# One-core graph layer: 8 KB adjacency runs, own rows gathered ahead of spilled ones, the spilled product and the eviction moved to the end of the period

## Reference

```python
h = jnp.maximum(_layernorm(x, axis=-1), 0.0)
mask = adj > 0
head = mask / jnp.maximum(jnp.sqrt(jnp.sum(mask * mask, axis=-1, keepdims=True)), 1e-12)
inc = adj + head
out = x + (inc @ h) / jnp.sum(inc, axis=-1, keepdims=True)
```

## Time and profile before

| | us |
|---|---|
| median of 3 runs (1261.79 to 1265.77) | 1264.53 |
| the profiled execution | 1265.03 |
| its span, first to last instruction | 1263.2 |
| busy: PE / DVE / ACT / POOL | 970.4 / 1162.8 / 977.8 / 764.9 |
| mean granted TensorE clock | 0.908 |

### The profile page before, as it was taken

One profiled execution on the slowest core, in us unless ns is written; L12 is line 12 of the kernel. 1 busy time (PEld: TensorE's weight loads), 2 busy tenths in 40 slices (PEclk: granted clock), 3 DMA queues, 4 the chain that ended last, 5 costly groups with the idle time before them and its releaser, 6 DMA issues.

```text
span 1263.2 us, 14630 instructions
## 1 busy us (share of the span) xinstructions
PE 970.4 (77%) x2678; PEld 482.8 (38%) x2678; DVE 1162.8 (92%) x2794; ACT 977.8 (77%) x1903; POOL 764.9 (61%) x745
## 2 busy tenths in 40 slices
PE   0002889988888888888888888798888878878676
PEld 0001334444444434444433444344444434434343
DVE  6679999999999999999998999989999989998972
ACT  6657888898888887888887787788878778876551
POOL 1003666766666667676666666775666667667453
PEclk9999999888889999889988988988899889998698
DMA  9999999999999999999999999999999999999442
GB/s 360 428 421 406 398 402 392 392 394 399 396 391 402 401 399 398 384 401 394 384 398 368 400 398 391 388 395 373 402 400 400 385 382 387 398 399 355 142 143 79
DMA packets 148127, 471.29 MB, mean 373 GB/s; under 512 B 24386, under 2 KB 24386, under 8 KB 143876
## 3 DMA queue, kind: packets, MB, share of 16 engines
q1 hardware_dynamic: 90368, 331.38, 66.9%
q0 software_dynamic: 57664, 138.93, 29.9%
HBM read 490.21 MB, written 33.82 MB: 415 GB/s over the span
## 4 chain that ended last, share of the span: by engine, by line
DVE 45%; DMA 20%; issue 20%; ACT 5%; SPq 5%; another core or an unknown queue 2%; PE 1%; DVEq 0%; ACTq 0%; POOL 0%; POOLq 0%
DMA adj_tile<-in_adj_dram 17%; DVE folded L774 15%; DVE cand_word L779 12%; DVE cand_index L783 5%; DMA gathered_rows<-in_x_dram 3%; SPq L385 2%; ACT junk L569 2%; DVE cand_word L797 2%; SPq L392 2%; DVE cand_index L802 2%; ACT adj_tile L556 2%; SPq L396 1%; DVE ln_stats L757 1%; DVE weights_and_payload L914 1%
## 5 line engine op out<-in xcount | busy, mean ns | idle before, releaser
L488 POOL DMA_INDIRECT gathered_rows<-h_scratch,slot_column x520 | 536.8, 1032 | 265.9 <-issue 161.2
L569 ACT ACTIVATE junk<-adj_tile,zero_unit 128x2048 bf16<-128x2048 f32 x256 | 510.1, 1994 | 111.2 <-issue 75.5
L1330 PE MATMUL acc<-gathered_rows,diag 128*128 128x512 f32 x1040 | 504.1, 641 | 0.5 <-issue 0.5
L488 POOL DMA_INDIRECT gathered_rows<-h_scratch,spill_column x197 | 220.5, 1119 | 199.0 <-ACT spill_column L615 150.8
L774 DVE SCALAR_TENSOR_TENSOR folded<-adj_tile 128x1024 f32<-128x1024 f32 x248 | 301.4, 1215 | 12.1 <-DMA adj_tile<-in_adj_dram 10.7
L1330 PEld LDWEIGHTS acc<-gathered_rows,diag 128*128 128x128 f32 x1040 | 213.7, 212 | 247.1 <-issue 246.8
L779 DVE MAX8 cand_word<-folded 128x8 f32<-128x1024 f32 x248 | 302.9, 1221 | 2.2
L783 DVE FIND_INDEX8 cand_index<-cand_word,folded 128x8 uint32<-128x1024 f32 x248 | 302.2, 1218 | 0.0
L1341 PE MATMUL acc<-gathered_rows,spill_matrix 128*128 128x512 f32 x394 | 186.3, 607 | 14.6 <-issue 10.7
L632 ACT ACTIVATE diag<-ident,weights_and_payload 128x128 f32<-128x128 f32 x582 | 176.2, 387 | 0.5 <-DVE weights_and_payload L914 0.5
L1278 PE MATMUL poff<-spill_rank,lanes_before 128*128 128x1 f32 x130 | 26.4, 272 | 187.5 <-DVE spill_rank L859 174.4
(11 more groups left out here) (146 smaller groups left out, 829.8 us busy)
## 6 DMA issues: line engine op xcount, KB each, us to landing
adj_tile<-in_adj_dram SPq DMA_DIRECT2D x256, 1024.0 KB
h_scratch<-adj_tile SPq DMA_DIRECT2D x16, 1024.0 KB, 10.5
out_dram<-out_tile SPq DMA_DIRECT2D x64, 256.0 KB
gathered_rows<-in_x_dram SPq DMA_DIRECT2D x12, 1024.0 KB, 12.6
x_residual<-in_x_dram SPq DMA_DIRECT2D x48, 256.0 KB
gathered_rows<-h_scratch,slot_column POOLq DMA_INDIRECT x520
x_held<-in_x_dram SPq DMA_DIRECT2D x4, 1024.0 KB, 7.9
gathered_rows<-h_scratch,spill_column POOLq DMA_INDIRECT x197
```

Of the source, the lines that this page charges most:

```text
L488: nc.gpsimd.indirect_dma_start(out=into, out_offset=None, in_=h[:, :], in_offset=bass.IndirectOffsetOnAxis(ap=column, axis=0), bounds_chec ...
L569: nc.scalar.activation(junk[:, n % 2].rearrange("p (j c) -> p j c", j=2), both[:, :, half], ACT.Relu, bias=zero_unit[:], scale=-UP, accum_ ...
L1330: last = nc.tensor.matmul(acc[t % 3][:], diag[:, t % 2, 1 + s], slot(t % 2, s), start=False, stop=False)
```

## The change

Four edits go together.

1. A chunk is now 2048 neighbouring columns, one run of 8 KB a row; the fold adds columns c and c + 1024 of the chunk. Bases, the diagonal's chunk and the order of the parts of an unfolded tile follow from it.
2. GpSimd gathers the own rows of tile T-1 before the spilled rows of tile T-3.
3. In a period TensorE does the own products right after the residual, then offsets, the payload, and the spilled product of tile f last.
4. ScalarE does `row_again` and `own_matrices` before the first check, `reach_places` right after the third, and evicts tile f at the end of the period. The store of a tile stands one period later in SyncE's queue.

The batch now has four spill groups in place of three, and one small step of the final tests is gone. In the last periods the gather of the batch's x rows stands later in GpSimd's list, and the batch period's eviction and spilled product of tile 60 stand later too.

```diff
-    adj_h = adj.rearrange("(c p j) (h n) -> c j p h n", p=P, j=ROWS, h=2)
+    adj_t = adj.rearrange("(c p j) n -> c j p n", p=P, j=ROWS)
...
         def diag_chunk(t):
-            return t // ROWS * P * ROWS % HALF // CW
+            return t // ROWS * P * ROWS // (2 * CW)
...
         def groups(t):
-            return EXTRA if FOLDED <= t < BATCH else FOLDED_EXTRA
+            return EXTRA if wide(t) else FOLDED_EXTRA
...
-                sp.dma_start(chunk(t % 2, j), adj_h[t // ROWS, t % ROWS, :, :, CW * j:CW * (j + 1)]).then_inc(adj_loaded[t % 2][j], 16)
+                sp.dma_start(A[:, t % 2, 2 * CW * j:2 * CW * (j + 1)],
+                             adj_t[t // ROWS, t % ROWS, :, 2 * CW * j:2 * CW * (j + 1)]).then_inc(adj_loaded[t % 2][j], 16)
...
-                if t >= 4:
-                    store_tile(t - 4)
+                if t >= 5:
+                    store_tile(t - 5)
...
-            gather_own(0)
-            gather_own(1)
-            for t in range(2, BATCH + 1):
+            for t in range(BATCH - 1):
...
-                gather_spill(t - 2)
-                if t < BATCH:
-                    gather_own(t)
+                gather_own(t)
+                if t >= 2:
+                    gather_spill(t - 2)
...
                 if pay:
-                    own_matrices(q)
                     if not wide(q):
                         row_again(q)
+                    own_matrices(q)
                 if t == FOLDED + 1:
                     list_rows()
+                check(t, 0)
...
-                if end:
-                    finish_tile(f)
                 if small:
                     reach_places(p)
                 check(t, 3)
+                if end:
+                    finish_tile(f)
...
-                if end:
-                    product_spill(f)
...
                 if pay:
                     residual(q)
+                    product_own(q, 0)
+                    product_own(q, 1)
                 offsets(p)
                 if pay:
                     bring_spill(q)
-                    product_own(q, 0)
-                if pay:
-                    product_own(q, 1)
+                if end:
+                    product_spill(f)
```

More of the change, by code:

```diff
@@ L206, in diag_chunk @@
         def diag_chunk(t):
-            return t // ROWS * P * ROWS % HALF // CW
+            return t // ROWS * P * ROWS // (2 * CW)
         def diag_column(t):
-            k = t // (TILES // 2) * 8 + t % 8
-            return diag_at[:, k:k + 1]
+            return diag_at[:, t % 16:t % 16 + 1]
         def cands(t):
@@ L242, in searched @@
             return CHUNKS * min(t, FOLDED) + PARTS * max(t - FOLDED, 0)
-        def part(i):
-            return i % 2 * CHUNKS + i // 2
         def paid(t, k):
@@ L422, in _ @@
                     load_chunk(t + 2, 3)
-            for t in range(TILES - 4, TILES):
+            for t in range(TILES - 5, TILES):
                 store_tile(t)
@@ L523, in _ @@
                         bounds_check=N - 1, oob_is_err=False).then_inc(batch_adj, 16)
-                    pool.wait_ge(row_added, FOLDED)
-                    nc.gpsimd.indirect_dma_start(
-                        out=again[:], out_offset=None, in_=x[:, :],
-                        in_offset=bass.IndirectOffsetOnAxis(ap=bad_row[:, 0:1], axis=0),
-                        bounds_check=N - 1, oob_is_err=False).then_inc(batch_x, 16)
-                gather_spill(t - 2)
-                if t < BATCH:
-                    gather_own(t)
+                gather_own(t)
+                if t >= 2:
+                    gather_spill(t - 2)
+            pool.wait_ge(row_added, FOLDED)
+            nc.gpsimd.indirect_dma_start(
+                out=again[:], out_offset=None, in_=x[:, :],
+                in_offset=bass.IndirectOffsetOnAxis(ap=bad_row[:, 0:1], axis=0),
+                bounds_check=N - 1, oob_is_err=False).then_inc(batch_x, 16)
+            gather_spill(BATCH - 3)
+            gather_own(BATCH - 1)
+            gather_spill(BATCH - 2)
             gather_spill(BATCH - 1)
@@ L683, in period @@
                     spill_matrix(r)
-                if small:
-                    roots(p)
                 if pay:
@@ L688, in period @@
                 check(t, 1)
+                if small:
+                    roots(p)
                 check(t, 2)
-                if end:
-                    finish_tile(f)
                 if small:
@@ L708, in batch_period @@
                 reach_places(y)
+                finish_tile(u)
                 check_batch(1)
@@ L786, in part_columns @@
             def part_columns(t, i):
-                if t == BATCH:
-                    return A[:, 0, CW * part(i):CW * (part(i) + 1)]
-                return chunk(t % 2, part(i) % CHUNKS)[:, part(i) // CHUNKS]
+                return A[:, t % 2, CW * i:CW * (i + 1)]
             def part_values(t, i):
@@ L794, in part_values @@
                 else:
-                    dve.wait_ge(adj_loaded[t % 2][part(i) % CHUNKS], 16 * turn(t))
-                e = slice(8 * part(i), 8 * part(i) + 8)
+                    dve.wait_ge(adj_loaded[t % 2][i // 2], 16 * turn(t))
+                e = slice(8 * i, 8 * i + 8)
                 nc.vector.max(out=cv[:, t % 2, e], in_=part_columns(t, i)).then_inc(vals_found, 1)
@@ L1177, in mark_rows @@
                                                     scalar=float(PLACES), in1=w_well[:, 5], op0=ALU.is_le, op1=ALU.add))
-                step(nc.vector.scalar_tensor_tensor(out=w_well[:, 6, TILES - FOLDED:], in0=end_all[:, BATCH:BATCH + 1],
-                                                    scalar=float(FOLDED_EXTRA * P),
-                                                    in1=w_well[:, 5, TILES - FOLDED:], op0=ALU.is_le, op1=ALU.add))
                 step(nc.vector.tensor_scalar(b_mark[:, FOLDED:], w_well[:, 6, 0:TILES - FOLDED], 4.5, None, ALU.is_lt))
@@ L1391, in batch_period @@
                 product_own(w, 1)
+                product_spill(u)
                 find_owner(y)
```

11 lines of the change are left out of this document (4 added, 7 removed).

## The result

The change makes the kernel slower: 1402.96 us in the median of 4 runs (1394.59 to 1408.27) against 1264.97, a ratio of 1.109, 95% interval 1.1032 to 1.1148. I had predicted 1259 us, and the range ended at 1281. The profiled execution of the changed kernel took 1394.59 us, its span is 1392.9.

What follows compares the result with a forecast made beforehand. VectorE bounds tiles 3 to 19, transfers plus payload waits tiles 20 to 60. With the new ring setting the period, +3.0, -9.4, -0.6 and +1.1 us give -5.9 from 1265.0: 1259 us, range 1244 to 1281.

Steps and rivals of the forecast that it cites:

- The ring: Loop from TensorE's spilled product through ScalarE's eviction, row_again and own_matrices to TensorE's next products; floors every period, taken as 17.15 us.
- The two ends are 16.2 and 17.35. I take 17.15: Ring length with TensorE at full rate, with its whole clock loss inside, and the value chosen near the upper end.
- The loss to TensorE's clock: TensorE's time at 1.2 GHz in the ring: about 1.15 us a period, not all of it counted.
- The handover from TensorE to ScalarE: From TensorE's last spilled pass to ScalarE's eviction in the ring; the ring's sum gave it no time.
- The long waits of `find_entry`: VectorE's waits for TensorE's payload, three in tiles 20 to 60, 13 us together; expected to be gone.
- The slack: Limits stand ready before VectorE reads them at pay_places: 5.0 us, spent once, taken off tiles 3 to 19.
- 8 KB runs: Adjacency loads: 0.31 us less per tile, bounds 0 and 0.5; transfers' pace in tiles 20 to 60 from 17.07 to 16.76.
- Rival C: Own-row gathers held back by longer runs: 0.4 us late a period, ring 17.55, about 1283 us; chance 0.08.
- Own rows first on GpSimd: Own gathers start up to 3.9 us earlier, spilled ones some 10 to 12 us later; no cost.
- Rival B: The ring binds with TensorE's whole clock loss: 17.45 us a period, 1276 us, slower; chance 0.20.
- the forecast: Ring near 17.15 us sets the period, time 1248 to 1268 us; chance 0.47.
- The end: Closing chain after the folded tiles: fourth spill group adds some 1.1 us; later eviction and product cost nothing.

Runs made afterwards that it cites:

- the fillers: Changed kernel with seven unread 256-column matmuls a period added on TensorE, in its waits: 1379.53 us, ratio 1.0835.
- runs8k_four_groups: Kernel before with 8 KB runs and the batch's four spill groups, all orders as before: 1275.49 us, ratio 1.0051.
- scalar_order_only: Kernel before with ScalarE's new order and the later store, nothing else: 1269.93 us, ratio 1.0007.
- scalar_as_before: Changed kernel with ScalarE's order and the store's place put back as before: 1664.3 us, ratio 1.318.
- own_gathers_first: runs8k_four_groups with GpSimd's new order and nothing else: 1390.92 us, ratio 1.0954.
- both excesses removed: Changed kernel with six unread TensorE matmuls a period and spilled gathers behind the closing: 1307.87 us, ratio 1.0331; with 4 KB runs 1279.8 us, 1.0104.

## Why the prediction was wrong

**The mechanism was right, its size was not.** The ring decides, it lies where the prediction put it, and its shortest turn is 16.14 us where 16.2 were worked out. The step that failed is the sentence "The two ends are 16.2 and 17.35. I take 17.15". The mean turn is 19.32. Of the 2.2 us between, 0.95 are the clock's (1.9 where 0.95 had been taken) and 1.3 the handover's. Two terms of the sum were mis-sized:

- *The loss to TensorE's clock.* I priced it at 1.15 us, the average loss of the kernel before, and took part of it off because time at the lower rate that falls on a wait "costs nothing". It is the other way round. The ring makes TensorE stand still for 1.76 and 2.20 us, and the diagonal product and the first own products behind that run at the lower level: 2.08 us for two passes in place of 1.10. The loss is 1.9 us, all of it in the ring, and the fillers removed all of it. The granted clock fell from 0.91 to 0.87 and 0.85. The Trainium skill (TensorE: Matmul & The Clock Gate, Why this matters for your kernels) advises against idle gaps between bursts of matmuls because the clock falls behind them; the trace agrees in direction, with 0.87 and 0.85 without fillers and 0.95 with them, though the two gaps here, 1.76 and 2.20 us, are shorter than those that the page warns of.
- *The handover from TensorE to ScalarE.* I priced it at nothing. It takes 0.63 us from the start of the last pass at best and 1.89 in the mean; the 1.3 us more come from GpSimd's gathers. In the folded periods of the kernel before nobody stood waiting for `acc_ready`, so no row of its waits showed it; its trace does record 40 of 50 closings as told of over 0.2 us late, and 1.5 us is the mean of all 50. The long waits of `find_entry` were a sign that TensorE's signals can be late; I left them at their place and did not ask what else waits for one.

The 58 periods took 319.90 + 798.10 = 1118.0 us; the prediction gave them 58 x 17.15 - 5.0 = 989.7. These 128 us, with 6.4 at the end and 1.2 in the first tiles, are its error of 135.5 in the profiled execution (1394.6 against 1259.1).

**The slack.** I took 5.0 us from the limits that `pay_places` reads. VectorE ran into `root` first; the diff moved `roots` behind the second check, and the prediction did not price that move.

**8 KB runs.** The gain of 0.31 us a tile is not there: 1.0051 (1.0018 to 1.0084) with the runs and the fourth group alone. Of the bounds, 0 was the better one, and a loss had not been allowed for. Rival C named the reason to look at, gathers that land later behind longer runs: 8.7 us in place of 6.2, 2.5 us more where the rival's sum had 0.4. In the changed kernel itself it is 6.6, and TensorE waits for gathered rows 7.0 us in all (2.4, 2.4 and 2.2), so C does not hold there; where the order is the old one, in runs8k_four_groups, its late gathers do show (68.5 us of waits). The Trainium skill (DMA: Bandwidth & Descriptors, Queues, rings and completion order) says that an engine finishes a packet before it turns to another queue; the later landing agrees with that, and no run here shows the order of service itself.

**Own rows first on GpSimd** was called "no cost". In the changed kernel that is so, because the spilled product goes last; by itself it costs 9%. The edits hold one another up, and edit 2 could not have been judged alone.

**Rival B** had the sign and the mechanism, and at 17.45 us a period it was 1.8 us short. It had 0.20 of the chances, against 0.47 for the forecast.

**The end** was put at +1.1 us for the fourth group; runs8k_four_groups shows 137.8 against 136.9, so that was right. The changed kernel has +7.5; the other 6.6 us lie in the moved steps, which had been put at nothing, and were not taken apart (scalar_order_only, with ScalarE's order and the later store alone, has 140.8).

## What to carry to other kernels

Before steps are moved in lists that run in strict order, follow the path once round a period: if it returns to its start in the next one, its whole length is a floor, and every handover and every wait on it has to be priced. In such a ring an engine's average loss to its clock is no price, since the ring creates the very gap behind which the clock falls; take the rows at the lower level. A part of a change that costs nothing in its company can cost as much as the whole when tried alone, so try the parts in both ways, alone and left out.

## What the runs showed that I had not expected

TensorE's signals can arrive late beside a burst of GpSimd's indirect gathers. The changed kernel's trace has the signal of 51 closings beside a burst. Of those that fall due (0.61 us after the start of the last pass, their best) from 5 us ahead of the start of the burst's last gather to 2.3 us behind it, 36 of 43 come over 0.2 us late, by up to 3.9 us, half of them 0.5 to 1.5 us after that gather's issue has ended; of the other eight none is late. Moving three gathers behind the closing took 1.26 us out of the last part of the turn, and 0.70 and 1.25 us out of the periods of the two stretches.

A burst alone does not do it. In scalar_as_before the closing falls into the same place (the last gather is issued 1.68 us after the start of the spilled product, 1.47 in the changed kernel), yet in the turn shown above the eviction starts 2.77 us after the product's start in place of 4.00 us, and 47 of 60 such signals are on time:

```profile
1003.97 2.74 PE L1334 MATMUL acc<-gathered_rows,spill_matrix 128*128 128x512 f32 x6
```

```profile
1005.65 1.00 POOL L485 DMA_INDIRECT gathered_rows<-h_scratch,spill_column  x1 [0.30 <-issue]
```

```profile
521.33:1500.80 979.47, 666.17 (x1682) 307.54 (x1681) 683.79 (x1600) 577.42 (x1148) 467.06 (x452) 0.79 0.80 286
```

The DMA share is 0.80 there in place of 0.95, but in own_gathers_first, where the share in the 3 us ahead of most such closings is over 0.93, only 6 of 22 are late. What GpSimd and TensorE share, and what else it takes, is open.

Runs twice as long made the kernel slower in two of three pairs: 0.5% for the runs and the fourth group, 2.2% with both excesses removed (1307.87 against 1279.8); with the ring in place (1402.96 against 1392.38, not timed side by side) the difference is within the runs' spread.
